# Two 16-head attention stages: who spreads the keys over the heads, and how values and mask enter

## Chip, cores and metric

The kernel is one program on one core of a Trainium2 chip. It is a chain of eight stages (four attention layers, each followed by a feed-forward layer) over 64 sequences of 64 tokens with 256 features; the activations `x` stay in SBUF from the first stage to the last. The metric is the device time of one execution in microseconds. The engines are TensorE (PE), VectorE (DVE), ScalarE (ACT), GpSimd (POOL) and the queue of SyncE (SP), which only issues DMAs.

## The reference, cut to what matters

Two of the attention layers have 16 heads of 16 features and attend from each sequence's 64 tokens to its 64 context tokens. The first (stage 0) quantizes the inputs of its query and output projections to 8 bits; the other (stage 6) has a gate and a mask of context tokens.

```python
# stage 0
q = _w8a8_linear(x, wq, bq).reshape(B, N, H, D).transpose(0, 2, 1, 3)
k = (cond @ wk.T + bk).reshape(B, L, H, D).transpose(0, 2, 1, 3)
v = (cond @ wv.T + bv).reshape(B, L, H, D).transpose(0, 2, 1, 3)
scores = jnp.einsum('bhnd,bhld->bhnl', q, k) * inv_sqrt_d + mask[:, None]
attn = jax.nn.softmax(scores, axis=-1)
o = jnp.einsum('bhnl,bhld->bhnd', attn, v)
...
return _w8a8_linear(o, wo, bo)
# stage 6
attn = jnp.einsum('blhd,bmhd->bhlm', q, k) * scale
attn = jnp.where(memory_mask[:, None, None, :], attn, -jnp.inf)
attn = jax.nn.softmax(attn, axis=-1)
...
out = out @ wo.T
gate = jax.nn.sigmoid(x @ wg.T)
return gate * out
```

## The kernel before

`head_attention_stage` builds both stages: "att8" with `quant=True` (stage 0) and "att32" with `quant=False` (stage 6). The work is cut into 16 units (`NU`) of 256 tokens, which is four sequences, and each unit into two groups (`GU` = 2) of 128 tokens, which is two sequences. All tiles are named `att_...` in the profile.

For a group, `scores_pe` (L2267) makes the scores of all 16 heads in two PSUM banks. It first lays the mask there with two matmuls against the identity (L2278), and then adds four products of queries and keys (L2284). A head has only 16 features, so eight heads at a time share one matmul: the keys `kT` are copied once for each of eight heads and multiplied by the head's 0/1 mask `hmask`. This spread copy is `km`; `keys_pool` (L2150) makes it on POOL in two instructions of 128x2048 elements (L2156). `max_dve` (L2297) takes the row maxima of each head, `exp_act` (L2308) does 16 exponentials, one for a head (L2311), `transpose_pe` (L2314) and `transposed_act` (L2322) turn the result, `apply_pe` (L2331) multiplies it by the values, `result_dve` (L2344) divides by the sums (and, in att8, quantizes: L2365, L2373), `result_pe`, `result_act` and `out_pe` turn it again and multiply by the output weights, and `residual_dve` (L2410) adds it to `x`.

For the unit after, PE makes in between the transposed inputs (`input_pe`, L2168), the keys (`keys_pe`, L2137), the queries (`queries_pe`, L2190 or L2195), the values (`values_pe`, L2227) and in att32 the gate (`gate_pe`, L2255). In att8 `queries_dve` (L2206, L2211) scales the queries on VectorE and `transposed_queries_pe` (L2247) turns them. The context `ctxT` is held twice in a row (its fourth dimension, `j`), so that one values matmul of 128 context rows gives one sequence's values in both halves of the partitions; a unit needs 8 of these matmuls of 256 columns. `values_act` copies them to the block tile `vbd`, even heads from the lower half and odd ones from the upper.

The order of the work is written out by hand, for each engine, in `unit_pe` (L2468), `unit_act` (L2501), `unit_dve` (L2530) and `unit_gp` (L2547). Every engine runs its own list in order; semaphores tie them. The groups overlap in a software pipeline: while the scores of group (t, g) are made, group k = 1 steps back is transposed and applied, k = 2 steps back its result is turned, and k = 3 steps back it is projected and added. The matmuls that make the unit after use two PSUM banks `FB` in turn, six fillings a unit, each waiting until ACT or VectorE has emptied the one before; in att32 the gate is the sixth (`LAST`), after the values. `apply_pe` waits for `y_used` of the group two before, since that group's output stands in the same bank.

`norm_dve` (L2073) normalizes the inputs two units ahead, with powers taken on POOL (`norm_pool`); `bias_pool` (L2404) adds the output bias to `x` in att8 after that. SP loads a unit's context with four DMAs (L2455), two units ahead.

## Time and profile before

| | |
|---|---|
| time, median of 3 runs | 5494.57 us (5493.93 to 5498.47) |
| profiled execution | 5491.58 us, its core's span 5489.8 us |
| PE busy | 4827.4 us, 88% |
| VectorE busy | 2886.1 us, 53% |
| ACT busy | 2072.0 us, 38% |
| POOL busy | 1154.1 us, 21% |
| granted clock of PE, mean | 0.938 |
| L2156 on POOL (the spread, both stages) | 64 instructions, 233.7 us |

| stretch | length | PE busy | VectorE busy | ACT busy | POOL busy | PE clock |
|---|---|---|---|---|---|---|
| att8, 37 to 500 us | 463 us | 347.05 | 348.58 | 205.90 | 150.76 | 0.86 |
| att32, 4370 to 4800 us | 430 us | 378.45 | 187.76 | 215.53 | 148.61 | 0.96 |

The first table is the whole program; the second is the two stages in question. Busy time says how long instructions ran on an engine, and that includes time in which a running instruction was held up. A clock of 1.00 is 2.4 GHz and 0.50 is 1.2 GHz; what stands between is a mean over both. In a timeline row the number in brackets is how long the engine stood idle before the row, and who ended it.

### The profile page before, as it was taken

The numbers are of one execution on the slowest core, as the hardware profiler recorded it, in microseconds if no ns is written. First come the engines' busy times: TensorE is split into PE (matmuls) and PEld (weight loads), VectorE is DVE, ScalarE is ACT, GpSimd is POOL, SyncE is SP. The second block draws the span as 40 slices with busy tenths as digits, with TensorE's granted clock in tenths as the row PEclk, the third lists the DMA queues.
The fourth block names the chain that finished last, engine by engine and source line by source line (L and its number), as shares of the span: only waits on it lengthen the run. The fifth ranks groups of instructions, "written<-read, shape, count | busy, mean of one in ns | idle before, by whom it ended". The sixth has DMA issues, their size and how long they took to land. (4 is left out here: it accounts for less than half of the span.)

```text
span 5489.8 us, 77694 instructions
## 1 busy us (share of the span) xinstructions
PE 4827.4 (88%) x27056; PEld 3829.2 (70%) x27056; DVE 2886.1 (53%) x5919; ACT 2072.0 (38%) x4822; POOL 1154.1 (21%) x758
## 2 busy tenths in 40 slices
PE   5776999998877748999999987999899899889999
PEld 3554899997656626777777776777677666567777
DVE  6776888895553245555555553333333244443333
ACT  3444666663214313333333333332333255443322
POOL 3332323331003300000000001222222243222222
PEclk9887999999989858999999998999899999999999
DMA  2001000000010011000000001000100011010000
GB/s 63 22 21 41 1 0 0 0 0 19 15 41 1 16 48 62 5 4 4 4 1 3 4 5 56 8 8 5 50 12 8 20 24 23 21 42 9 5 8 8
DMA packets 130897, 94.20 MB, mean 17 GB/s; under 512 B 77200, under 2 KB 114160, under 8 KB 130448
## 3 DMA queue, kind: packets, MB, share of 16 engines
q1 hardware_dynamic: 130704, 91.65, 5.6%
q8 instruction: 119, 1.95, 0.2%
q14 instruction: 74, 0.61, 0.0%
HBM read 83.23 MB, written 8.39 MB: 17 GB/s over the span
## 5 line engine op out<-in xcount | busy, mean ns | idle before, releaser
L1152 POOL TENSOR_TENSOR peer_tab<-peer_sims 128x2048 f32<-128x2048 f32 x64 | 245.8, 3860 | 290.0 <-ACT peer_sims L1129 260.4
L1145 ACT ACTIVATE peer_tab<-peer_sims 128x128 f32<-128x128 f32 x1024 | 305.6, 392 | 0.0
L1200 DVE SCALAR_TENSOR_TENSOR peer_tab<-peer_tab,peer_th 128x2048 f32<-128x2048 f32 x128 | 298.3, 2373 | 2.6 <-ACT peer_tab L1145 2.3
L2156 POOL TENSOR_TENSOR att_km<-att_kT,att_hmask 128x2048 f32<-128x2048 f32 x64 | 233.7, 3673 | 247.6 <-ACT att_kT L2146 247.6
L643 DVE TENSOR_TENSOR moe_b<-moe_a,bank 128x512 f32<-128x512 f32 x128 | 88.1, 688 | 370.1 <-PE bank L556 348.3
L631 POOL TENSOR_TENSOR moe_hh_lo<-moe_hh,moe_hh_hi 128x512 fp32r<-128x512 f32 x128 | 171.5, 1340 | 499.0 <-ACT moe_hh_hi L622 479.0
L1217 PE MATMUL bank<-ident,peer_tab 128*128 128x128 f32 x2048 | 247.7, 275 | 23.2 <-DVE peer_tab L1200 23.2
L1217 PEld LDWEIGHTS bank<-ident,peer_tab 128*128 128x128 f32 x2048 | 234.5, 142 | 36.4 <-DVE peer_tab L1200 24.0
L1267 PE MATMUL bank<-peer_wd,peer_hh 128*128 128x256 f32 x1024 | 242.1, 380 | 1.7 <-DVE peer_hh L1258 1.7
L1240 PE MATMUL bank<-peer_hT,peer_wg 128*128 128x256 f32 x1024 | 243.3, 381 | 0.0
L1708 PE MATMUL bank<-mha_wo,mha_oT 128*128 128x256 f32 x1024 | 242.5, 380 | 0.0
L1595 PE MATMUL bank<-mha_wv,mha_hT 128*128 128x512 f32 x512 | 240.4, 592 | 0.0
L643 DVE TENSOR_TENSOR moe2a_b<-moe2a_a,bank 128x512 f32<-128x512 f32 x104 | 71.5, 688 | 295.3 <-PE bank L556 272.6
L631 POOL TENSOR_TENSOR moe2a_hh_lo<-moe2a_hh,moe2a_hh_hi 128x512 fp32r<-128x512 f32 x104 | 141.1, 1356 | 400.1 <-ACT moe2a_hh_hi L622 386.1
L2311 ACT ACTIVATE att_pr<-bank,att_nmax 128x64 f32<-128x64 f32 x1024 | 216.3, 377 | 2.2 <-DVE att_nmax L2306 2.1
L1240 PEld LDWEIGHTS bank<-peer_hT,peer_wg 128*128 128x128 f32 x1024 | 196.4, 192 | 26.2
L643 DVE TENSOR_TENSOR moe2b_b<-moe2b_a,bank 128x512 f32<-128x512 f32 x96 | 66.0, 688 | 272.8 <-PE bank L556 249.9
L631 POOL TENSOR_TENSOR moe2b_hh_lo<-moe2b_hh,moe2b_hh_hi 128x512 fp32r<-128x512 f32 x96 | 130.8, 1362 | 373.2 <-ACT moe2b_hh_hi L622 366.2
L1267 PEld LDWEIGHTS bank<-peer_wd,peer_hh 128*128 128x128 f32 x1024 | 188.7, 191 | 24.1 <-DVE peer_hh L1258 2.3
L1708 PEld LDWEIGHTS bank<-mha_wo,mha_oT 128*128 128x128 f32 x1024 | 185.7, 191 | 19.5
L622 ACT ACTIVATE moe_hh_hi<-moe_hh 128x512 fp32r<-128x512 f32 x128 | 80.9, 632 | 301.2 <-DVE moe_hh L648 301.2
L1616 DVE COPY mha_ks<-bank 128x512 f32<-128x512 f32 x128 | 88.5, 691 | 198.8 <-PE bank L1583 191.5
(485 smaller groups left out, 12675.0 us busy)
## 6 DMA issues: line engine op xcount, KB each, us to landing
att_ctxT<-in_ctxT_dram SPq DMA_DIRECT2D x128, 128.0 KB, 2.5
x<-in_x_dram SPq DMA_DIRECT2D x4, 1024.0 KB, 9.3
lin_ctxT<-in_ctxT_dram SPq DMA_DIRECT2D x16, 256.0 KB, 2.8
mem_ctxT<-in_ctxT_dram SPq DMA_DIRECT2D x16, 256.0 KB, 2.9
mem_ctx<-in_ctx_dram SPq DMA_DIRECT2D x16, 256.0 KB, 3.0
t_scratch<-mha_tT SPq DMA_DIRECT2D x8, 512.0 KB, 2.7
moe2a_hTf<-t_scratch SPq DMA_DIRECT2D x8, 512.0 KB, 3.6
moe2b_hTf<-t_scratch SPq DMA_DIRECT2D x8, 512.0 KB, 3.7
```

The costliest lines, as they stand in the source:

```text
L631: nc.gpsimd.tensor_tensor(out=hhs[1][:, j % 2, :], in0=hh[:, j % 2, :], in1=hhs[0][:, j % 2, :], op=ALU.subtract).then_inc(lo_ready, 1)
L643: nc.vector.tensor_tensor(out=b[:, j % 2, :], in0=a[:, j % 2, :], in1=U[j % 2][:], op=ALU.mult).then_inc(b_ready, 1)
L1145: i = nc.scalar.activation(tab[g][h][:, b * P:(b + 1) * P], sims[:, g, h, P:2 * P], ACT.Identity, bias=sims[:, g, h, b:b + 1])
L1152: nc.gpsimd.tensor_tensor(out=tab[g][h][:].rearrange("p (a b) -> p a b", b=P), in0=sims[:, g, h, P:2 * P].unsqueeze(1).broadcast_to([P, NB ...
L1200: nc.vector.scalar_tensor_tensor(out=tab[g][h][:], in0=tab[g][h][:], scalar=th[:, g, h:h + 1], in1=tab[g][h][:], op0=ALU.is_ge, op1=ALU.mu ...
L1217: i = nc.tensor.matmul(TB[n % 2][:, j * P:(j + 1) * P], tab[g][h][:, blk * P:(blk + 1) * P], core.ident[:], start=(j == 0 and h == 0), sto ...
L1240: i = nc.tensor.matmul(GB[p % 2][:, n * PU:(n + 1) * PU], wg[:, c, blk * P:(blk + 1) * P], hT[par][:, c, :], start=(c == 0), stop=(c == C ...
L1267: i = nc.tensor.matmul(YB[par][:, g * D:(g + 1) * D], hh[:, p % 2, n * PU + g * P:n * PU + (g + 1) * P], wd[:, 2 * p + n, :], start=(p == ...
L1595: i = nc.tensor.matmul(V[:], hT[:, c, g * P:(g + 1) * P], wv[:, c, first * HD:(first + QUAD) * HD], start=(c == 0), stop=(c == C - 1))
L1708: i = nc.tensor.matmul(Y[g // 2][:, (g % 2) * D:(g % 2 + 1) * D], oT[:, s % 2, g * P:(g + 1) * P], wo[:, s, :], start=(s == 0 and g % 2 == ...
L2156: i = nc.gpsimd.tensor_tensor(out=km[par][:, c, :, :, :], in0=kT[:, c, :].rearrange("p (b k) -> p b k", k=S).unsqueeze(2).broadcast_to([P, ...
L2311: i = nc.scalar.activation(pr[g][:, h, :], SB[g][h // H8][:, (h % H8) * S:(h % H8 + 1) * S], ACT.Exp, bias=nmax[:, g, h:h + 1])
```

## The change

Five things change in `head_attention_stage`, for both stages where nothing else is said.

- The spread of the keys leaves POOL. In att8 its first half (`KM_ACT`, features 0 to 127) goes to ACT as 8 activations, one for a head with the head's mask as scale (`spread_act`), and its second half to VectorE as one 128x2048 multiply (`spread_dve`). In att32 both halves go to VectorE.
- The context is held once. One values matmul makes the values of two sequences, one in each half of the partitions, so a unit takes 4 matmuls instead of 8; `values_act` copies them, partly from one half of the partitions to the other, with 8 activations instead of 4. SP issues one context DMA for a unit instead of four.
- In att32 the mask no longer goes through PE. `max_dve` adds it while it moves the scores from PSUM to the SBUF tile `pr` (two adds for a group), then takes one maximum over `pr`, and the exponentials read `pr`.
- The order moves: `queries_pe` stands before `apply_pe` and `result_pe`; `queries_dve` before `result_dve`; the spreads come after `result_act` on ACT and after `result_dve` on VectorE.
- On POOL, `bias_pool` comes before `norm_pool`.

```diff
--- before.py
+++ after.py
...
-    ctxT = [sb(f"ctxT{i}", [P, C, BU, 2, S]) for i in range(2)]
+    ctxT = [sb(f"ctxT{i}", [P, C, UNIT]) for i in range(2)]
...
+    KM_ACT, KM_DVE = ((0,), (1,)) if quant else ((), (0, 1))
+    km_act, km_dve = sem("km_act"), sem("km_dve")
...
-                i = nc.tensor.matmul(F[:, co * UNIT:(co + 1) * UNIT], wkT[:, ci, co * P:(co + 1) * P], ctxT[par][:, ci, :, 0, :],
+                i = nc.tensor.matmul(F[:, co * UNIT:(co + 1) * UNIT], wkT[:, ci, co * P:(co + 1) * P], ctxT[par][:, ci, :],
...
-        if some(t):
-            act.wait_ge(km_ready, t)
+        if some(t * len(KM_DVE)):
+            act.wait_ge(km_dve, t * len(KM_DVE))
+        if some(t * len(KM_ACT)):
+            act.wait_ge(km_act, t * len(KM_ACT))
...
-    def keys_pool(pool, t, par):
-
-        pool.wait_ge(emptied[KEYS % 2], t * 3 + KEYS // 2 + 1)
+    def spread_act(act, t, par):
+
         if some((t - 1) * GU):
-            pool.wait_ge(scored, (t - 1) * GU)
-        for c in range(C):
-            i = nc.gpsimd.tensor_tensor(out=km[par][:, c, :, :, :],
-                                        in0=kT[:, c, :].rearrange("p (b k) -> p b k", k=S).unsqueeze(2).broadcast_to([P, BU, H8, S]),
-                                        in1=hmask[:].unsqueeze(1).unsqueeze(3).broadcast_to([P, BU, H8, S]), op=ALU.mult)
-        i.then_inc(km_ready, 1)
+            act.wait_ge(scored, (t - 1) * GU)
+        act.wait_ge(emptied[KEYS % 2], t * 3 + KEYS // 2 + 1)
+        for c in KM_ACT:
+            for h in range(H8):
+                i = nc.scalar.activation(km[par][:, c, :, h, :], kT[:, c, :].rearrange("p (b k) -> p b k", k=S), ACT.Copy,
+                                         scale=hmask[:, h:h + 1])
+            i.then_inc(km_act, 1)
+
+    def spread_dve(dve, t, par):
+
+        if some((t - 1) * GU):
+            dve.wait_ge(scored, (t - 1) * GU)
+        dve.wait_ge(emptied[KEYS % 2], t * 3 + KEYS // 2 + 1)
+        for c in KM_DVE:
+            nc.vector.tensor_tensor(out=km[par][:, c, :, :, :],
+                                    in0=kT[:, c, :].rearrange("p (b k) -> p b k", k=S).unsqueeze(2).broadcast_to([P, BU, H8, S]),
+                                    in1=hmask[:].unsqueeze(1).unsqueeze(3).broadcast_to([P, BU, H8, S]),
+                                    op=ALU.mult).then_inc(km_dve, 1)
...
-        for b in range(2):
-            for c in range(C):
-                tok = ctxT[par][:, c, 2 * n + b, :, :].rearrange("p j k -> p (j k)")
-                i = nc.tensor.matmul(F[:, b * D:(b + 1) * D], tok, wvT[:, c, :],
-                                     start=(c == 0), stop=(c == C - 1))
+        for c in range(C):
+            i = nc.tensor.matmul(F[:, 0:D], ctxT[par][:, c, n * P:(n + 1) * P], wvT[:, c, :], start=(c == 0), stop=(c == C - 1))
...
-        v = FB[k % 2][:].rearrange("p (b h j d) -> p b h j d", b=2, j=2, d=HD)
-        for j in range(2):
-            i = nc.scalar.activation(vbd[par][64 * j:64 * j + 64, 2 * n:2 * n + 2, :, j, 0:HD], v[64 * j:64 * j + 64, :, :, j, :], ACT.Copy)
+        v = FB[k % 2][:, 0:D].rearrange("p (h j d) -> p h j d", j=2, d=HD)
+        for b in range(2):
+            for j in range(2):
+                i = nc.scalar.activation(vbd[par][64 * j:64 * j + 64, 2 * n + b, :, j, 0:HD], v[64 * b:64 * b + 64, :, j, :], ACT.Copy)
...
-            if not quant:
-                pe.wait_ge(neg_ready, t + 1)
...
-        for c in range(C):
-            nc.tensor.matmul(SB[g][c][:].rearrange("p (h k) -> p h k", k=S), core.ident[:],
-                             add[:, g, :].unsqueeze(1).broadcast_to([P, H8, S]), start=True, stop=False, skip_group_check=True)
+        if quant:
+            for c in range(C):
+                nc.tensor.matmul(SB[g][c][:].rearrange("p (h k) -> p h k", k=S), core.ident[:],
+                                 mask[par][:, g, :].unsqueeze(1).broadcast_to([P, H8, S]), start=True, stop=False, skip_group_check=True)
         if g == 0:
-            pe.wait_ge(km_ready, t + 1)
+            if KM_ACT:
+                pe.wait_ge(km_act, (t + 1) * len(KM_ACT))
+            pe.wait_ge(km_dve, (t + 1) * len(KM_DVE))
         for c in range(C):
             for b in range(2):
                 i = nc.tensor.matmul(SB[g][c][64 * b:64 * b + 64, :], qT[par][:, c, (2 * g + b) * S:(2 * g + b + 1) * S],
-                                     km[par][:, c, 2 * g + b, :, :].rearrange("p h k -> p (h k)"), start=False, stop=(b == 1),
+                                     km[par][:, c, 2 * g + b, :, :].rearrange("p h k -> p (h k)"), start=not quant, stop=(not quant or b == 1),
                                      skip_group_check=True)
...
         kp = keep[:, bass.ds(t * GU, GU), :]
+        m_chain.begin(t)
         nc.vector.tensor_reduce(out=valid[:, par, :], in_=kp, axis=AX.X, op=ALU.max)
-        if some((t - 1) * GU):
-            dve.wait_ge(scored, (t - 1) * GU)
-        nc.vector.tensor_scalar(neg[par][:], kp, 1.0, BIG, ALU.subtract, ALU.mult).then_inc(neg_ready, 1)
-
-    def max_dve(dve, t, g):
+        nc.vector.tensor_scalar(neg[par][:], kp, 1.0, BIG, ALU.subtract, ALU.mult).then_inc(m_chain.sem, 1)
+        dve.wait_ge(m_chain.sem, m_chain.next())
+
...
-        for c in range(C):
-            i = nc.vector.tensor_reduce(out=nmax[:, g, c * H8:(c + 1) * H8], in_=SB[g][c][:].rearrange("p (h k) -> p h k", k=S),
-                                        axis=AX.X, op=ALU.max)
-        i.then_inc(soft_chain.sem, 1)
+        if quant:
+            for c in range(C):
+                i = nc.vector.tensor_reduce(out=nmax[:, g, c * H8:(c + 1) * H8], in_=SB[g][c][:].rearrange("p (h k) -> p h k", k=S),
+                                            axis=AX.X, op=ALU.max)
+            i.then_inc(soft_chain.sem, 1)
+        else:
+            if some(n - 1):
+                dve.wait_ge(pT_ready, n - 1)
+            for c in range(C):
+                i = nc.vector.tensor_tensor(out=pr[g][:, c * H8:(c + 1) * H8, :], in0=SB[g][c][:].rearrange("p (h k) -> p h k", k=S),
+                                            in1=neg[par][:, g, :].unsqueeze(1).broadcast_to([P, H8, S]), op=ALU.add)
+            i.then_inc(s_read, 1)
+            dve.wait_ge(s_read, n + 1)
+            nc.vector.tensor_reduce(out=nmax[:, g, :], in_=pr[g][:], axis=AX.X, op=ALU.max).then_inc(soft_chain.sem, 1)
         dve.wait_ge(soft_chain.sem, soft_chain.next())
...
-            i = nc.scalar.activation(pr[g][:, h, :], SB[g][h // H8][:, (h % H8) * S:(h % H8 + 1) * S], ACT.Exp, bias=nmax[:, g, h:h + 1])
+            s_ = SB[g][h // H8][:, (h % H8) * S:(h % H8 + 1) * S] if quant else pr[g][:, h, :]
+            i = nc.scalar.activation(pr[g][:, h, :], s_, ACT.Exp, bias=nmax[:, g, h:h + 1])
...
-    n_in, n_ctx = 16 * len(loads), 16 * (2 * C + (1 if quant else 0))
+    n_in, n_ctx = 16 * len(loads), 16 * (1 + (1 if quant else 0))
...
-        for c in range(C):
-            for j in range(2):
-                sp.dma_start(ctxT[par][:, c, :, j, :], src[:, c, :].rearrange("p (b k) -> p b k", k=S)).then_inc(ctx_in[par], 16)
+        sp.dma_start(ctxT[par][:], src).then_inc(ctx_in[par], 16)
...
@@ -2478,14 +2500,13 @@
             if g == 0 and exists(t + 1):
                 input_pe(pe, t + 1)
                 keys_pe(pe, t + 1, nxt)
+                queries_pe(pe, t + 1, nxt)
             if g == 1 and quant and exists(t + 1):
                 transposed_queries_pe(pe, t + 1)
             if exists(t1):
                 apply_pe(pe, t1, p1, g1)
             if exists(t2):
                 result_pe(pe, t2, g2)
-            if g == 0 and exists(t + 1):
-                queries_pe(pe, t + 1, nxt)
             if g == 1 and exists(t + 1):
...
-            if g == 0 and not quant and exists(t + 1):
-                q_copy(act, t + 1, nxt, QUERIES)
+            if g == 0 and exists(t + 1):
+                if not quant:
+                    q_copy(act, t + 1, nxt, QUERIES)
+                if KM_ACT:
+                    spread_act(act, t + 1, nxt)
...
             if exists(t):
-                max_dve(dve, t, g)
+                max_dve(dve, t, par, g)
             if exists(t3):
                 residual_dve(dve, t3, p3, g3)
+            if g == 0 and quant and exists(t + 1):
+                queries_dve(dve, t + 1)
             if exists(t1):
                 result_dve(dve, t1, p1, g1)
-            if g == 0 and quant and exists(t + 1):
-                queries_dve(dve, t + 1)
+            if g == 0 and exists(t + 1):
+                spread_dve(dve, t + 1, nxt)
             if g == 1 and not quant and exists(t + 1):
                 neg_dve(dve, t + 1, nxt)
             if g == 1 and exists(t + 2):
                 norm_dve(dve, t + 2)
 
     def unit_gp(pool, t, par):
-        if exists(t + 1):
-            keys_pool(pool, t + 1, 1 - par)
+        if quant and exists(t + 1):
+            bias_pool(pool, t + 1)
         if exists(t + 2):
             norm_pool(pool, t + 2)
-        if quant and exists(t + 1):
-            bias_pool(pool, t + 1)
...
```

## Rows read from the trace of the kernel before

**Rows 1.** Timeline, att8: start us, us, engine, line, instruction, [idle before <- releaser].

```profile
206.83 1.93 PE L2340 MATMUL bank<-att_vbd,att_pT 128*64 128x34 f32 x32 [1.49 <-DVE x L2422]
...
222.54 7.38 POOL L2156 TENSOR_TENSOR att_km<-att_kT,att_hmask 128x2048 f32<-128x2048 f32 x2 [7.47 <-ACT att_kT L2146]
...
222.66 0.60 PE L2190 MATMUL bank<-att_wqT,att_hT 128*128 128x256 bf16 x4
...
223.40 3.04 DVE L2365 TENSOR_TENSOR att_o<-att_o,att_bv 128x256 f32<-128x256 f32 x1
...
232.54 1.09 PE L2247 MATMUL bank<-ident,att_qf 128*128 128x128 f32 x4 [4.49 <-DVE att_qf L2211]
...
235.11 1.93 PE L2340 MATMUL bank<-att_vbd,att_pT 128*64 128x34 f32 x32 [1.49 <-DVE x L2422]
```

**Rows 2.** VectorE groups, 80 to 448 us: line, instruction, count, busy us, mean ns, idle.

```profile
L2365 DVE TENSOR_TENSOR att_o<-att_o,att_bv 128x256 f32<-128x256 f32 x27 | 44.7, 1655 | 0.9
...
L2088 DVE SCALAR_TENSOR_TENSOR att_xn<-x,att_mv,att_rstd 128x256 f32<-128x256 f32 x26 | 24.5, 980 | 10.6 <-POOL att_rstd L2122 10.6
...
L2350 DVE RECIPROCAL att_rsum<-bank 128x16 f32<-128x16 f32 x27 | 7.0, 258 | 51.6 <-PE bank L2340 51.6
```

**Rows 3.** Stretches of 1 us, att8: busy times; third from the end PEclk.

```profile
230.00:231.00 1.00, 0.00 (x0) 0.00 (x0) 0.87 (x3) 0.00 (x0) 0.00 (x0) 0.65 0.87 197
...
240.00:241.00 1.00, 1.00 (x5) 0.86 (x4) 0.85 (x5) 0.18 (x1) 0.00 (x0) 0.73 0.00 0
```

**Rows 4.** Timeline, att32: PE's order through a unit, and two VectorE rows.

```profile
4522.04 1.88 PE L2278 MATMUL bank<-att_neg,ident 128*128 128x512 f32 x4
...
4530.41 3.62 PE L2227 MATMUL bank<-att_wvT,att_ctxT 128*128 128x256 f32 x16
...
4533.87 1.89 PE L2255 MATMUL bank<-att_wgT,att_hT 128*128 128x256 f32 x8
...
4535.60 1.88 PE L2278 MATMUL bank<-att_neg,ident 128*128 128x512 f32 x4
...
4537.41 1.94 PE L2284 MATMUL bank<-att_km,att_qT 128*64 128x512 f32 x8
...
4539.27 1.13 PE L2401 MATMUL bank<-att_woT,att_oT 128*128 128x256 f32 x4
...
4539.39 1.29 DVE L2302 TENSOR_REDUCE att_nmax<-bank 128x8 f32<-128x512 f32 x2 [2.99 <-PE bank L2284]
...
4541.12 0.60 PE L2168 MATMUL bank<-ident,att_xn 128*128 128x128 f32 x4
...
4541.53 0.43 DVE L2426 SCALAR_TENSOR_TENSOR x<-att_y,x 128x256 f32 x1 [0.17 <-DVE att_y L2424]
4541.55 1.89 PE L2137 MATMUL bank<-att_ctxT,att_wkT 128*128 128x256 f32 x8
...
4543.38 1.13 PE L2340 MATMUL bank<-att_vbd,att_pT 128*64 128x34 f32 x32
...
4544.71 1.89 PE L2195 MATMUL bank<-att_hT,att_wqT 128*128 128x256 f32 x8
...
4546.44 1.88 PE L2278 MATMUL bank<-att_neg,ident 128*128 128x512 f32 x4
```

**Rows 5.** VectorE groups, 4420 to 4736 us (13 units of att32).

```profile
L2353 DVE TENSOR_SCALAR att_rsum<-att_rsum,att_valid 128x16 f32<-128x16 f32 x26 | 43.5, 1671 | 0.9
L2302 DVE TENSOR_REDUCE att_nmax<-bank 128x8 f32<-128x512 f32 x52 | 33.5, 686 | 61.4 <-PE bank L2284 61.4
...
L2350 DVE RECIPROCAL att_rsum<-bank 128x16 f32<-128x16 f32 x26 | 6.7, 258 | 60.8 <-PE bank L2340 60.8
```

**Rows 6.** Groups of the whole program: prices of forms that the change adds.

```profile
L172 DVE TENSOR_TENSOR ffn_wg_lo<-ffn_dq_wg,ffn_wg_hi 128x2048 fp32r<-128x2048 f32 x1 | 2.3, 2293 | 2.0 <-ACT ffn_wg_hi L177 2.0
...
L1145 ACT ACTIVATE peer_tab<-peer_sims 128x128 f32<-128x128 f32 x1024 | 305.6, 392 | 0.0
L2311 ACT ACTIVATE att_pr<-bank,att_nmax 128x64 f32<-128x64 f32 x1024 | 216.3, 377 | 2.2 <-DVE att_nmax L2306 2.1
```

More of the change, by code:

```diff
@@ L2026, in head_attention_stage @@
     emptied = [sem(f"emptied{i}") for i in range(2)]
-    km_ready, scored, m_ready, e_ready = (sem(n) for n in ("km_ready", "scored", "m_ready", "e_ready"))
+    scored, s_read, m_ready, e_ready = (sem(n) for n in ("scored", "s_read", "m_ready", "e_ready"))
     pT_ready, pTs_ready, o_ready = (sem(n) for n in ("pT_ready", "pTs_ready", "o_ready"))
@@ L2049, in head_attention_stage @@
         neg, valid = [sb(f"neg{i}", [P, GU, S]) for i in range(2)], sb("valid", [P, 2, GU])
-        neg_ready = sem("neg_ready")
         ms_ready, ms_eps, r1_raw, rr_ready = sem("ms_ready"), sem("ms_eps"), sem("r1_raw"), sem("rr_ready")
         norm_chain = Chain(sem("norm_chain"), 3)
+        m_chain = Chain(sem("m_chain"), 1)
     INPUT, KEYS, QUERIES = range(3)
@@ L2268, in scores_pe @@
         n = t * GU + g
-        add = mask[par] if quant else neg[par]
         QK = LAST if quant else QUERIES
         if g == 0:
-            if not quant:
-                pe.wait_ge(neg_ready, t + 1)
             pe.wait_ge(emptied[QK % 2], t * 3 + QK // 2 + 1)
@@ L2291, in neg_dve, with max_dve @@
         kp = keep[:, bass.ds(t * GU, GU), :]
+        m_chain.begin(t)
         nc.vector.tensor_reduce(out=valid[:, par, :], in_=kp, axis=AX.X, op=ALU.max)
-        if some((t - 1) * GU):
-            dve.wait_ge(scored, (t - 1) * GU)
-        nc.vector.tensor_scalar(neg[par][:], kp, 1.0, BIG, ALU.subtract, ALU.mult).then_inc(neg_ready, 1)
-    def max_dve(dve, t, g):
+        nc.vector.tensor_scalar(neg[par][:], kp, 1.0, BIG, ALU.subtract, ALU.mult).then_inc(m_chain.sem, 1)
+        dve.wait_ge(m_chain.sem, m_chain.next())
+    def max_dve(dve, t, par, g):
         n = t * GU + g
```

## Prediction

> **What bounds the kernel now.** I read the views in this order: the page's slices (TensorE 88% busy overall, but 50 to 90% in the first stage), then the timeline of one unit in each of the two stages the change touches, then the groups of VectorE (DVE) in steady units, then the granted clock around TensorE's (PE's) pauses. Only these two stages change: "att8" (16 units) and "att32" (16 units).
>
> In att8 a unit takes 235.11 - 206.83 = 28.28 us. PE stands idle 4.49 us for `att_qf` and 1.49 us for `x`, both from VectorE [rows 1]. VectorE is late because GpSimd (POOL) spreads the keys meanwhile: the 128x256 add of L2365, met 0.9 us after L2156 started, took 3.04 us [rows 1]. Its mean is 1.655 us [rows 2], though 128x256 elements should take 0.42 us: an estimate from 2048 elements in 2.293 us and 512 in 0.686 us [rows 5, 6], 1.05 ns an element. L2373 is hit in the same way; L2088 runs into POOL's bias add, mean 0.98 for 0.42 by the same estimate. VectorE itself is held up by PE only at L2350, 51.6 us in 27 calls, so 3.8 us a unit [rows 2]. So att8 is a VectorE queue of some 24.5 us with two short waits. PE's pauses bring it down to the lower of its two clock levels: the 1 us stretch of the drop shows 0.65, the one of the rise 0.73 [rows 3], and 235.11 to 240.7 ran at 1.2 GHz, although PE was dense from 235.11.
>
> In att32 a unit takes 4546.44 - 4522.04 = 24.40 us [rows 4] and PE runs nearly without a gap. VectorE waits for PE 61.4 + 60.8 us in 13 units, so 9.4 us a unit, and loses 2.9 us to POOL at L2353 (43.5 us in 26 calls, where a 128x16 operation needs about 0.23) [rows 5]. So att32 is bound by PE, and work moved from POOL and PE to VectorE lands on an engine with some 12.1 us of work (24.40 - 9.4 - 2.9).
>
> **att8, part by part.** (1) POOL's spread goes (2 x 3.67 us). The stalls of L2365 and L2373 go with it: 2 x 2 x (1.655 - 0.42) = 4.9 us a unit. The bias add now starts right behind `xn_ready`, beside the maxima, which read PSUM: L2088's 2 x 0.56 = 1.1 us a unit goes too. (2) Half the spread (128x2048) lands on VectorE. The nearest row is the two-input 128x2048 form, 2.293 us [rows 6]. Bounds: 1.2 us if it ran at two elements a cycle, 3.7 us if it took what POOL takes [rows 1]. I take 2.3. Both inputs are broadcast views, which I price at nothing. (3) The other half is 8 activations of 128x256 on ScalarE (ACT): L1145's 128 elements cost 305.6/1024 = 0.30 us each [rows 6], so 0.4 for 256 (estimate, 0.83 ns an element more), 3.2 us a unit. They stand ahead of the copy of the transposed scores. Counted from the end of scores(t,0): keys copied at 3, exponentials 3.4, a result copy 0.4, spread 3.2, transposed copy 1.1, so 11.2; the step that needs it, `apply`, also needs VectorE's second residual, which ends at 12.4 (2.57, queries 1.8, result 3.2, spread 2.3, 2.57). Hidden; without that cover up to 3.2 us a unit. (4) Values: 4 matmuls of 256 columns in place of 8, 3.46 to 1.73 us of PE (start to start, 4530.41 to 4533.87) [rows 4]; ACT gets 8 pieces in place of 4, +0.8 us a unit at most. PE has room: nothing. (5) Queries move ahead of `apply`, and VectorE's query step ahead of its result step, so `qf` no longer comes behind the stalls and the 4.49 us pause goes. (6) 4 context DMAs become 1; nobody waits for them in a steady unit: nothing.
>
> Sum: 28.28 - 3.8 - 4.9 - 1.1 + 2.3 = 20.8 us of VectorE queue. Two waits remain. The first is before the query step: PE's input 0.43, keys 1.83 [rows 4], queries 0.60 [rows 1] and 0.1 of signalling against VectorE's maximum and residual, 2.57 us (4539.39 to 4541.53 + 0.43) [rows 4]: 0.4 us. The second is `apply`, which can't begin before VectorE's residual: 0.3 of signalling plus 1.1 us (1.13 at full clock, 1.93 at the lower, [rows 1, 4]), 1.4 to 2.3. So 22.6 to 23.5 us. PE still has two pauses of about 2 to 2.6 us a unit, and some will cost clock just when VectorE waits for input, keys and queries (up to 2.9 us more). I take 24.0. Fifteen such steps: 15 x 4.3 = 64 us gained (range 35 to 84).
>
> **att32, part by part.** Removed from PE: 4 mask matmuls, 2 x 1.81 us, and half the values, 1.73 [rows 4], leaving some 19 us less its old pause, about 17.6. Added to VectorE: both halves of the spread, 2 x 2.29; four adds of the mask, each 0.69 (priced by the 128x512 maximum that also reads PSUM, 0.686 [rows 5]; bounds 0.5 and 1.1); the one wait behind them 0.1. The maximum over 1024 SBUF elements costs what two over 512 PSUM elements did. The stall of L2353 goes. VectorE's queue is 12.1 + 4.6 + 2.8 + 0.2 = 19.7 us.
>
> But queue and PE take turns here. Count from the moment scores(t,0) are done. PE: output and transposes 1.85, input 0.43, keys 1.83, queries 1.73, apply 1.05, with 0.3 of signalling: 7.2 us [rows 4]. Only then can VectorE do result(t-1,1), about 1.0, then both spreads 4.6, then the maximum and residual of the second group, 2.57 + 1.4 = 3.95: 16.7. Behind that residual stands `apply(t,0)` on PE, and behind `apply` everything else. PE had finished its second scores and transposes by about 11: a pause of over 5 us. Then follow at full clock 0.2, apply and result 1.33, values 1.73, gate 1.73, scores 1.86. That alone gives 23.6. ACT however starts the second exponentials only when that maximum is ready (15.7); 16 of them cost 3.4 us from PSUM (216.3/1024 each), under 4.8 by L1145 [rows 6], and from SBUF I take 3.9; a result copy of 256 elements about 0.4, the first values copy 4 x 0.3 = 1.2, and only then is the bank free for `gate`: 21.2 + 1.73 + 1.86 = 24.8 us.
>
> With a pause of 5 us I expect the lower clock. In att8 4.49 us idle gave it, and it lasted 5.6 us into dense work [rows 1, 3]. Apply to values then take twice 3.06, until 23.0, and gate and scores follow mostly at the upper level: 26.6 us, 2.2 more than now. Fifteen steps: 33 us lost (range: 7 lost at full clock, 60 lost).
>
> The Trainium skill (TensorE: Matmul & The Clock Gate, section on HAM oscillation in real kernels) says that a loop which leaves TensorE waiting in each pass restarts each pass at the lower clock. This case's trace agrees at the 4.49 us pause of att8. By that rule att32's unit is the 26.6 us, without it the 24.8. The skill (VectorE: DVE Perf Modes, section on SBUF-source operations) also gives ScalarE 52 cycles more for a source in SBUF than in PSUM; by it the 16 exponentials would take 3.4 + 0.7 = 4.1 us, an estimate, where I took 3.9, and the full-clock unit 25.0.
>
> Heads and tails of the stages: the first spread gets shorter (3 us each), the last units get the adds on their chain (3 us). Nothing. Total: 5491.6 - 64 + 33 = 5460.6 for the profiled execution, which lay 3.0 us under the median of the runs. Forecast 5463.
>
> **Rivals.**
> A. The clock stays up in att32, or the pause is shorter than counted. Unit 24.4 to 24.8 us, stage 0 to 7 us lost; total 5430. For it: full clock through all of att32 now, and pauses of 1.4 us do no harm. Against: my pause is 5 us. Chance 0.20.
> B. Both stages do better: in att32 the VectorE chain sets the pace at 23.6 or less, because the adds or the spread are cheaper than their rows. Total 5405. Chance 0.06.
> C. Slower. In att32 the pause keeps PE at the lower level through gate and scores as well, in every unit, and the long loop of VectorE and PE feeds itself: 26.6 + 3.6 = 30.2 us less the part that is hidden, so 29 to 30; 15 x 5.2 = 78 us lost against 64 gained: 5508. It decides from a unit of 28.7 us on. For it: two engines in turns, and att8 now, with a similar share of pauses, loses 5 to 10 us a unit to the lower level. Against: there the level rose within dense work shorter than what att32 will have. Chance 0.13.
> D. The change doesn't do what it says in att8: the freed VectorE only swaps POOL's stalls for PE's lower clock and waits (26.5 us a unit), att32 as forecast: 5497. For it: the loop att8 has between VectorE and PE is kept. Against: the queue itself is 3.6 us shorter, and the longest pause is gone. Chance 0.10.
> My forecast: 0.51, by itself 5438 to 5485.
>
> **How the numbers follow.** 0.2% of this time is 11 us, about what a measurement of this kernel can tell from no change. Faster than 5484: nearly all of my case (0.48), A, B, a little of D: 0.76. Within: 0.03 of my case, most of D's rest: 0.11. Slower: C and nothing else: 0.13. The range leaves out B's lower half and C's upper half: 5408 to 5510.
>
> **What would show it.** att8: unit near 24, L2365 and L2373 near 0.42 and 0.48, no `att_qf` wait of 4 us, and the 128x2048 multiply near 2.3 us. att32: VectorE busy near 80%, PE pausing about 5 us before L2340's successor with `x` as releaser, a mean clock clearly below 1.00, unit 26 to 27. Wrong if the spread on VectorE costs over 3 us, if att32 keeps clock 1.00, or if att8's unit stays above 26.

## The result, and the profile after

| | before | after |
|---|---|---|
| time, median | 5496.52 us (5493.93 to 5498.85, 4 runs) | 5440.88 us (5438.93 to 5444.32, 4 runs) |
| profiled execution, its span | 5491.58 us, 5489.8 us | 5442.19 us, 5440.4 us |
| att8 with its head and tail | 457.8 us | 382.5 us |
| the stages between | 3886.7 us | 3890.8 us |
| att32 with its head and tail | 406.8 us | 426.8 us |

The changed kernel takes 0.99 of the time before (95% interval 0.9882 to 0.9917), 56 us less. In the two profiled executions the difference is 49.4 us of span: att8 gives 75.3, att32 costs 20.0, the rest 5.9. The stage lengths are differences of starts: from a stage's first `xn` (L2090 in att8, at 36.8 before and 37.3 after; L2117 in att32) to the first statistics of the stage behind it. The view of who reads `x`, after (form, count, least/mean/greatest ns, first to last start):

```profile
L1048 DVE BATCH_NORM_STATS2 peer_stats<-x x32: 407/416/427, 419.8 to 1137.6; 128x6 f32 x24, 128x6 f32<-128x256 f32 x8
...
L2117 DVE SCALAR_TENSOR_TENSOR att_xn<-x,att_mv,att_rr x32: 477/482/486, 4310.6 to 4677.9; 128x256 f32<-128x256 f32 x32
L287 DVE BATCH_NORM_STATS2 moe_stats<-x x32: 407/409/427, 4737.4 to 5276.9; 128x6 f32<-128x256 f32 x16, 128x6 f32 x16
```

419.8 - 37.3 is att8, 4737.4 - 4310.6 is att32. The same rows give the lengths of all kernels below.

The timeline of one unit of att8, after, which answers to [rows 1]:

```profile
203.69 1.73 PE L2364 MATMUL bank<-att_vbd,att_pT 128*64 128x34 f32 x32 [3.05 <-DVE x L2446]
...
205.46 0.26 DVE L2374 RECIPROCAL att_rsum<-bank 128x16 f32<-128x16 f32 x1 [2.12 <-PE bank L2364]
...
217.03 0.88 DVE L2221 SCALAR_TENSOR_TENSOR att_qf<-bank,att_sx,att_swq 128x256 f32<-128x256 f32 x2 [0.40 <-PE bank L2205]
...
219.41 0.42 DVE L2389 TENSOR_TENSOR att_o<-att_o,att_bv 128x256 f32<-128x256 f32 x1
...
220.71 0.48 DVE L2397 SCALAR_TENSOR_TENSOR att_o<-att_o,att_rso,att_fixed 128x256 f32<-128x256 f32 x1
220.72 3.42 ACT L2161 ACTIVATE att_km<-att_kT,att_hmask 128x256 f32<-128x256 f32 x8
...
221.57 2.28 DVE L2171 TENSOR_TENSOR att_km<-att_kT,att_hmask 128x2048 f32<-128x2048 f32 x1
...
223.91 1.20 ACT L2352 ACTIVATE att_pT<-bank 128x512 f32<-128x512 f32 x2
...
226.58 1.13 PE L2364 MATMUL bank<-att_vbd,att_pT 128*64 128x34 f32 x32 [3.03 <-DVE x L2446]
...
227.76 3.62 PE L2240 MATMUL bank<-att_wvT,att_ctxT 128*128 128x256 f32 x8
```

The unit is 226.58 - 203.69 = 22.89 us. The adds that took 3 us beside POOL take 0.42, half the spread takes 2.28 on VectorE and 3.42 on ACT. VectorE stands still for PE twice, 2.12 us for `apply` (1.51 in the next unit, where `apply` ran at the full clock) and 0.40 for the queries. From 80 to 380 us it waits 25.0 us for `apply` in 27 groups, so 1.9 us a unit (group: count, busy us, mean ns, idle before):

```profile
L2374 DVE RECIPROCAL att_rsum<-bank 128x16 f32<-128x16 f32 x27 | 6.9, 254 | 25.0 <-PE bank L2364 25.0
```

The same view of one unit of att32, after, which answers to [rows 4]:

```profile
4472.62 1.94 PE L2297 MATMUL bank<-att_km,att_qT 128*64 128x512 f32 x8
...
4481.63 0.26 DVE L2374 RECIPROCAL att_rsum<-bank 128x16 f32<-128x16 f32 x1 [3.13 <-PE bank L2364]
...
4482.62 4.48 DVE L2171 TENSOR_TENSOR att_km<-att_kT,att_hmask 128x2048 f32<-128x2048 f32 x2
...
4487.02 1.28 DVE L2323 TENSOR_TENSOR att_pr<-bank,att_neg 128x512 f32<-128x512 f32 x2
...
4489.80 3.93 ACT L2335 ACTIVATE att_pr<-att_pr,att_nmax 128x64 f32<-128x64 f32 x16 [2.93 <-DVE att_nmax L2329]
...
4491.01 1.88 PE L2364 MATMUL bank<-att_vbd,att_pT 128*64 128x34 f32 x32 [5.26 <-DVE x L2450]
...
4493.30 2.50 PE L2240 MATMUL bank<-att_wvT,att_ctxT 128*128 128x256 f32 x8
...
4494.97 2.30 ACT L2252 ACTIVATE att_vbd<-bank 64x128 f32<-64x128 f32 x8 [0.98 <-PE bank L2240]
...
4496.16 1.99 PE L2268 MATMUL bank<-att_wgT,att_hT 128*128 128x256 f32 x8 [0.36 <-ACT att_vbd L2252]
...
4498.09 1.94 PE L2297 MATMUL bank<-att_km,att_qT 128*64 128x512 f32 x8
```

Here the unit is 4498.09 - 4472.62 = 25.47 us, against 24.40. PE stands 5.26 us for `x`, because VectorE makes both halves of the spread (4.48 us), then the adds and the maximum, before it reaches that residual. Stretches of 1 us around the pause, and one of 220 us of the stage (length, busy us of PE, PE's weight loads, VectorE, ACT and POOL with their instructions, granted clock of PE, DMA share, GB/s):

```profile
4490.00:4491.00 1.00, 0.00 (x0) 0.02 (x1) 0.51 (x2) 1.00 (x5) 0.00 (x0) 1.00 0.00 0
4491.00:4492.00 1.00, 0.99 (x21) 1.00 (x22) 0.00 (x0) 1.00 (x6) 0.00 (x0) 0.55 0.00 0
...
4494.00:4495.00 1.00, 1.00 (x5) 0.80 (x5) 0.86 (x5) 0.03 (x1) 0.00 (x0) 0.74 0.00 0
...
4420.00:4640.00 220.00, 176.13 (x1254) 125.83 (x1252) 135.33 (x263) 130.06 (x447) 15.71 (x35) 0.90 0.04 11
```

The clock still stands at 1.00 (2.4 GHz) at the end of the pause, falls to the lower level as the work comes back (0.55 in that microsecond), and rises halfway through the one from 4494 (0.74): some 3.4 us. This happens in every steady unit: twelve of them, counted from `gate` to `gate`, take 25.3 to 25.8 us.

### The profile page after: what moved, and what is told of

It is laid out like the page before. It is cut to its first block and busy times, and to the rows that moved or that the text cites. A ratio compares the mean times of both kernels' runs of the same rounds, so it can differ in the third digit from the quotient of the medians.

```text
span 5440.4 us, 77052 instructions
## 1 busy us (share of the span) xinstructions
PE 4748.9 (87%) x26672; PEld 3774.5 (69%) x26672; DVE 2897.5 (53%) x5999; ACT 2160.3 (40%) x5078; POOL 920.4 (17%) x694
## 5 line engine op out<-in xcount | busy, mean ns | idle before, releaser
L1217 PE MATMUL bank<-ident,peer_tab 128*128 128x128 f32 x2048 | 247.9, 275 | 24.4 <-DVE peer_tab L1200 24.4
L2364 PE MATMUL bank<-att_vbd,att_pT 128*64 128x34 f32 x2048 | 91.7, 253 | 127.1 <-DVE x L2450 62.6
L1609 ACT ACTIVATE mha_vs<-bank 128x512 f32<-128x512 f32 x128 | 76.4, 597 | 297.6 <-PE bank L1595 297.6
```

Source lines behind the costliest of these rows:

```text
L1217: i = nc.tensor.matmul(TB[n % 2][:, j * P:(j + 1) * P], tab[g][h][:, blk * P:(blk + 1) * P], core.ident[:], start=(j == 0 and h == 0), sto ...
L2364: i = nc.tensor.matmul(OB[g][64 * b:64 * b + 64, p * 2 * HV:(p + 1) * 2 * HV], pT[:, p, 64 * b:64 * b + 64], vbd[par][:, 2 * g + b, p, :, ...
```

## The experiments

All numbers are medians with their span, ratios are to the kernel before with their 95% interval. "After" has 5440.9 us.

**e1: the old att32 beside the new att8.** The stage function of before is kept under another name and called for att32.

```diff
-head_attention_stage(core, "att32", quant=False)
+head_attention_stage_before(core, "att32", quant=False)
```

> The changed kernel, with the second stage (att32) exactly as it was before the change; att8 changed. My account of the two traces is that att8 gained 75 us and att32 lost 20 us. If the stages are independent: att32 back at 407 us from 427, the whole 20 us faster than the changed kernel, about 5421. If some of att8's gain was only moved (a debt paid in later stages), the whole stays at 5435 to 5441.

5418.39 us (5416.37 to 5421.67), ratio 0.9863 (0.9847 to 0.988). att8 382.4, att32 409.0 us. att8 keeps its gain when att32 is the old one, so the stages can be taken one by one, as in all that follows. The median is 22 us below after's. In the profiled executions the span is 25 us shorter: 18 us are att32's, 5 lie between the stages (3885.6 us for 3890.8) and 2 behind them, which the edit doesn't touch.

**e2: att32's mask back on PE.** Four matmuls against the identity again, the maxima and exponentials straight from PSUM; the spread stays on VectorE.

```diff
-        if quant:
+        if True:
             for c in range(C):
                 nc.tensor.matmul(SB[g][c][:]..., core.ident[:],
-                                 mask[par][:, g, :]...
+                                 (mask if quant else neg)[par][:, g, :]...
```

> The changed kernel with att32's mask put back on PE (two matmuls a group) and the maxima and exponentials reading PSUM; the spread stays on VectorE. Loop theory (apply waits for VectorE's residual, which stands behind result, both spreads and the second maximum): the loop loses the adds, 1.4 us, but PE has 1.8 us more in the chain from gate to scores; PE's pause shrinks from 5.3 to about 2.5 us and the clock stays up; unit 24.0 to 24.7 against 25.47, 12 to 22 us faster. ScalarE theory (what costs is that exponentials read SBUF, 3.93 for 3.38 us): 0.55 us a unit, 9 us faster, with the pause as long as before. PE theory (any PE work given back costs): 3.6 us a unit, 58 us slower.

5430.06 us (5426.58 to 5434.96), ratio 0.9886 (0.987 to 0.9903); att32 418.7, 8 us less than after, and the whole 11 us less, just under what was expected. PE's pause halves as expected, but the clock holds in some units only. Timeline of e2, `apply` and `gate` of two units, and two stretches of the stage:

```profile
4430.88 1.13 PE L2367 MATMUL bank<-att_vbd,att_pT 128*64 128x34 f32 x32 [2.29 <-DVE x L2453]
...
4434.47 1.99 PE L2268 MATMUL bank<-att_wgT,att_hT 128*128 128x256 f32 x8 [0.37 <-ACT att_vbd L2252]
...
4581.76 1.13 PE L2367 MATMUL bank<-att_vbd,att_pT 128*64 128x34 f32 x32 [2.28 <-DVE x L2453]
...
4586.44 1.96 PE L2268 MATMUL bank<-att_wgT,att_hT 128*128 128x256 f32 x8
```

```profile
4362.00:4458.00 96.00, 85.89 (x607) 56.34 (x606) 51.94 (x111) 54.77 (x206) 6.60 (x15) 1.00 0.04 12
4460.00:4660.00 200.00, 180.99 (x1202) 120.48 (x1200) 103.25 (x221) 109.15 (x407) 13.90 (x31) 0.94 0.04 10
```

From `apply` to `gate` it is 3.59 us in the first unit and 4.68 in the second, behind the same pause. Counted from `gate` to `gate`, the four units of the first stretch take 24.2 to 24.4 us and the eight of the second 25.4 to 25.8. The first is what e4 takes below with the mask on VectorE and the clock at 1.00 (24.2 to 24.4), the second what after takes (25.3 to 25.8). So at an equal clock the place of the mask is worth nothing that can be measured: the mask's 1.88 us come back on PE in the loop and cancel what VectorE and ACT save. Most of the 8 us are the units in which the clock stayed up, five of them, 1.3 us each. Why it stayed up in those and not in the others, with pauses of 2.2 to 2.3 us in both, isn't shown.

**e3: att32's spread back on POOL**, the mask stays on VectorE. **e5: the same in att8**, all else new.

```diff
+    ON_POOL = not quant        # e5: ON_POOL = quant
+    if ON_POOL:
+        KM_ACT, KM_DVE = (), (0, 1)
...
+        for c in range(C):
+            nc.gpsimd.tensor_tensor(out=km[par][:, c, :, :, :], in0=kT..., in1=hmask..., op=ALU.mult)
```

> The changed kernel with att32's spread put back on POOL; the mask stays on VectorE. Loop theory: 4.6 us leave VectorE's part of the loop, some 1 to 2 us of stalls beside POOL come back (the 128x16 multiply, the residual with two SBUF inputs); the pause of PE shrinks to 1 to 2 us, the unit to 22.6 to 23.5, 30 to 45 us faster than the changed kernel, and att32 below its 407 us of before. ScalarE theory: the chain exponentials, result copy, values copy, gate, scores is as long as in the changed kernel, so within 5 us of it. Port theory (keeping POOL off SBUF is what matters): 30 us slower or more.

5390.91 us (5384.01 to 5393.82), ratio 0.9809 (0.9792 to 0.9825). att32 falls to 378.5 us, 28 us under the kernel before and 48 under after: slightly more than the loop theory said. Timeline of e3:

```profile
4480.39 7.21 POOL L2174 TENSOR_TENSOR att_km<-att_kT,att_hmask 128x2048 f32<-128x2048 f32 x2 [6.90 <-ACT att_kT L2153]
...
4482.65 1.40 DVE L2391 TENSOR_SCALAR att_rsum<-att_rsum,att_valid 128x16 f32<-128x16 f32 x1
...
4484.59 1.29 DVE L2337 TENSOR_TENSOR att_pr<-bank,att_neg 128x512 f32<-128x512 f32 x2
...
4488.87 1.93 PE L2378 MATMUL bank<-att_vbd,att_pT 128*64 128x34 f32 x32 [2.39 <-DVE x L2464]
```

POOL's 7.2 us lie beside VectorE's work. Of that one 128x16 operation with both inputs in SBUF is held up (1.40 us for 0.23 elsewhere), and by 0.3 us the 128x16 negation behind the maxima (L2343); the adds of the mask read PSUM and SBUF and take 1.29 us for two, as without POOL. The pause is 2.39 us and the unit 4495.85 - 4473.42 = 22.43. With the spread back on POOL att32 is also 30 us shorter than the old stage in e1 (409.0), so the rest of the change is a gain there. e7 prices the values; what the moved queries give in att32, and the mask's place beside a spread on POOL, have no run of their own.

> The changed kernel with att8's whole spread back on POOL; order, values and bias add as changed, att32 as changed. Stall theory (att8's gain is that POOL no longer holds up VectorE's two-input operations): VectorE loses its 2.3 us multiply but gets back two or three stalls of 1.5 to 3.3 us a unit; unit 24.5 to 27 against 22.89, 25 to 60 us slower than the changed kernel. Load theory (VectorE is simply the busiest engine of att8, the stalls are hidden by the new order): unit 20.6 to 22, 15 to 37 us faster. att32's run with the spread on POOL gained, so the second is to be taken seriously.

5503.0 us (5498.64 to 5511.03), ratio 1.0015 (1.0006 to 1.0025): att8 443.0 us, 60.5 more than after. Timeline of e5:

```profile
243.16 7.64 POOL L2174 TENSOR_TENSOR att_km<-att_kT,att_hmask 128x2048 f32<-128x2048 f32 x2 [7.26 <-ACT att_kT L2153]
...
243.55 3.78 DVE L2240 TENSOR_TENSOR att_qf<-att_qf,att_bq 128x512 f32<-128x512 f32 x1 [0.15 <-DVE att_qf L2235]
...
247.99 3.10 DVE L2403 TENSOR_TENSOR att_o<-att_o,att_bv 128x256 f32<-128x256 f32 x1
...
255.66 1.93 PE L2378 MATMUL bank<-att_vbd,att_pT 128*64 128x34 f32 x32 [6.63 <-DVE x L2460]
```

The stalls are back in the new order (3.78 us for the 0.69 of a 128x512 add, 3.10 for 0.42), and PE waits 6.63 us. The two stalls are 5.8 us a unit and the multiply that left VectorE 2.3, so 3.5 of the 4.0 us by which a unit grew (26.8 us from spread to spread). So of att8's 75 us, 60 are the spread that left POOL. The Trainium skill (SBUF — State Buffer, section on who interferes with whom) says that a VectorE instruction with two SBUF inputs contends with a GpSimd instruction that reads SBUF, and one with at most one such input, outside its two-port modes, doesn't. The rows of e5 agree for the first, the adds of e3 for the second. L2343 of e3 has one input in SBUF and took 299 ns on the mean for 175 after; no run here shows in which mode it ran.

**e4: fill the pause of att32.** Four idle matmuls of 512 columns, whose results serve nothing, into the free score banks, ahead of `apply(t,0)`.

```diff
+        if g == 0 and not quant:
+            for r in range(4):
+                nc.tensor.matmul(SB[g][r % 2][:], core.ident[:], wkT[:]..., start=True, stop=True, ...)
```

> The changed kernel with four matmuls of 512 columns that serve nothing, put in att32 ahead of apply(t, 0), into a scores bank that is free just then, in PE's pause of 5.3 us; nothing else differs. If the lower clock after the pause costs: apply back from 1.88 to 1.13 us, values copy no longer waiting 0.98 us for its matmuls, 0.6 to 1.0 us a unit, 10 to 16 us faster, granted clock of the stage near 1.00. If ScalarE's chain hides the lower clock: within 3 us. If the loop's length alone decides: within 3 us as well, with the clock at 1.00.

5422.25 us (5420.09 to 5425.36), ratio 0.9869 (0.9852 to 0.9885); att32 410.1, 17 us less. Timeline of e4:

```profile
4483.71 3.70 PE L2360 MATMUL bank<-att_wkT,ident 128*128 128x512 f32 x8 [1.18 <-ACT att_pT L2352]
...
4487.68 1.13 PE L2367 MATMUL bank<-att_vbd,att_pT 128*64 128x34 f32 x32 [0.28 <-DVE x L2453]
...
4491.85 1.99 PE L2268 MATMUL bank<-att_wgT,att_hT 128*128 128x256 f32 x8 [0.94 <-ACT att_vbd L2252]
```

The clock reads 1.00 over 220 us of the stage where it read 0.90. The unit is 24.37 us, so the lower level costs att32 1.1 us a unit (1.3 on the mean of the steady units, 25.6 and 24.3) and the longer loop nothing: at full clock the new att32 is as long as the old. After shows where the 1.1 goes: ACT waits 0.98 us for the slow values.

**e6: att8's old order.** Queries behind `apply` on PE, and VectorE's query step behind its result step.

```diff
                 keys_pe(pe, t + 1, nxt)
-                queries_pe(pe, t + 1, nxt)
...
+            if g == 0 and exists(t + 1):
+                queries_pe(pe, t + 1, nxt)
```

> The changed kernel with att8's query steps in the order of before: PE's queries behind apply and result, VectorE's query step behind its result step (ahead of the spread). If the moved order carried the gain: the pause of PE for the scaled queries comes back, 2 to 4 us a unit, 30 to 60 us slower. If the order matters little once the stalls are gone (VectorE does the same work, and only the 0.4 us wait for the queries moves): within 8 us of the changed kernel.

5452.24 us (5450.38 to 5453.85), ratio 0.9918 (0.9901 to 0.9935); att8 397.6 us, 15 more. Neither theory: the order is worth 11 to 15 us, about 1 us a unit. No long pause for `qf` comes back, and none is there in e5, with the stalls and the new order: the pause of before took both. The timeline of e6 has instead:

```profile
244.90 0.26 DVE L2374 RECIPROCAL att_rsum<-bank 128x16 f32<-128x16 f32 x1 [1.52 <-PE bank L2364]
...
254.55 1.93 PE L2364 MATMUL bank<-att_vbd,att_pT 128*64 128x34 f32 x32 [3.81 <-DVE x L2446]
```

VectorE waits 1.52 us for a product that in the new order is made while it works on the queries. The new order fills a hole in VectorE's queue. The three steps that were taken back one at a time, 60 by e5, 15 here and 5 by e7, add up to 80 us and not to 75, so they overlap a little.

**e7: values as before in both stages**, eight matmuls, four context DMAs and two copies of 64x256 for each pair of sequences.

```diff
-            i = nc.tensor.matmul(F[:, 0:D], ctxT[par][:, c, n * P:(n + 1) * P], wvT[:, c, :], ...)
+            for b in range(2): ... i = nc.tensor.matmul(F[:, b * D:(b + 1) * D], tok, wvT[:, c, :], ...)
```

> The changed kernel with the values made as before in both stages: context held twice, 8 matmuls and 4 copies a unit, 4 context DMAs. PE gets 1.73 us a unit more at full clock. In att8 VectorE sets the pace and PE has pauses: 0 to 5 us in the stage. In att32 the first half of the values takes 0.87 us more (1.7 at the lower clock) ahead of the copy that frees the gate's bank, while the copy itself is 0.35 us shorter: 0.5 to 1.4 us a unit, 8 to 22 us. Together 8 to 27 us slower. If PE's work is hidden in both: within 3 us.

5465.3 us (5464.03 to 5467.82), ratio 0.9944 (0.9928 to 0.9961); att8 +4.6, att32 +21.0 us, both within what was expected. In att32 values stand on the path behind the pause, at the lower level, and ACT's copy waits for them (timeline of e7):

```profile
4505.59 4.97 PE L2242 MATMUL bank<-att_wvT,att_ctxT 128*128 128x256 f32 x16
...
4508.87 0.79 ACT L2254 ACTIVATE att_vbd<-bank 64x256 f32<-64x256 f32 x2 [2.65 <-PE bank L2242]
```

4.97 us for 2.50: the halved values save 1.3 us a unit of att32, without which the stage would have lost 41 us rather than 20.

**e8: att32 with the spread split between ACT and VectorE as in att8, mask on PE.** The edit of e2, and `KM_ACT, KM_DVE = (0,), (1,)` for both stages.

> The changed kernel with att32 spread as att8 is (first half on ScalarE, second on VectorE) and with its mask back on PE. VectorE's part of the loop loses 2.3 us against the run with the mask on PE and the spread on VectorE. Loop theory with VectorE alone: unit 22 to 22.7, the whole near 5395. But ScalarE gets 3.4 us a unit ahead of the copy of the transposed scores and of the second exponentials, and PE has 1.8 us more between gate and scores: if that chain sets the pace, the unit stays at 24.0 to 24.7 and the whole at 5420 to 5430.

5423.31 us (5422.84 to 5426.29), ratio 0.9868 (0.9852 to 0.9885); att32 410.9 us. The numbers are those of the case in which ACT's chain takes over, but not by the reason given. Timeline of e8, and its group of transposed copies from 4420 to 4640 us (9 units):

```profile
4480.45 3.43 ACT L2161 ACTIVATE att_km<-att_kT,att_hmask 128x256 f32<-128x256 f32 x8
...
4485.81 3.40 ACT L2338 ACTIVATE att_pr<-bank,att_nmax 128x64 f32<-128x64 f32 x16
...
4486.16 1.13 PE L2367 MATMUL bank<-att_vbd,att_pT 128*64 128x34 f32 x32 [1.36 <-ACT att_pT L2355]
...
4490.46 1.99 PE L2268 MATMUL bank<-att_wgT,att_hT 128*128 128x256 f32 x8 [1.08 <-ACT att_vbd L2252]
```

```profile
L2355 ACT ACTIVATE att_pT<-bank 128x512 f32<-128x512 f32 x36 | 19.5, 594 | 53.0 <-PE bank L2345 53.0
```

VectorE had the maximum ready at 4484.4, but ACT starts the exponentials at 4485.8; PE waits for ACT at `apply` and at `gate`. ACT isn't late by its half of the spread: that ends at 4483.9, and ACT then stands idle for 0.96 us until PE's transposes are done, in each unit (53.0 us in 9 units, 5.0 and 0.96 us in each). The transposes come late because the mask is laid on PE ahead of the scores. So what sets the pace is a loop of PE and ACT: transposes, their copy, exponentials, values copy, `gate`, mask, scores. Against the units of e2 at full clock (24.2 to 24.4 us) e8's take 24.1 to 24.2, so 2.3 us less on VectorE gain some 0.2.

**e9: e3 with one idle matmul of 512 columns ahead of att32's `apply(t,0)`. e10: the same in att8 too.**

```diff
+        if g == 0 and not quant:   # e10: if g == 0
+            for r in range(1):
+                nc.tensor.matmul(SB[g][r % 2][:], core.ident[:], wkT[:]..., ...)
```

> The run with att32's spread on POOL, with one matmul of 512 columns that serves nothing in att32's pause ahead of apply(t, 0). That run kept a pause of 2.4 us and a lower clock behind it: apply 1.93 for 1.13 us, and the values copy waited 0.88 us for its matmuls. If both go, as four such matmuls did in the longer pause: unit 21.4 to 21.8 against 22.43, 10 to 16 us faster than that run, near 5377. If one matmul is too little to hold the clock: within 3 us of it.

5378.16 us (5376.97 to 5382.74), ratio 0.9786 (0.977 to 0.9802), 13 us under e3: the fastest of all. The stretch of 4420 to 4640 us, e3 and then e9 (columns as in the stretches above):

```profile
4420.00:4640.00 220.00, 194.41 (x1432) 139.01 (x1432) 126.01 (x288) 149.66 (x516) 88.07 (x60) 0.92 0.04 11
```

```profile
4420.00:4640.00 220.00, 197.69 (x1493) 133.16 (x1490) 132.58 (x298) 153.79 (x533) 94.27 (x62) 1.00 0.04 11
```

0.92 becomes 1.00, and the unit goes from 22.43 to 21.44 us. Two units of e3's own trace ran at 1.00, and they took 21.4 us too; its others, in the middle of the stage, 22.1 to 22.6.

> As the run before it, and the same one matmul in att8's pause too. att8's queue on VectorE includes the wait for apply, which takes 1.73 to 1.93 us at the lower clock in some units and 1.13 in others: 0 to 0.8 us a unit, 3 to 10 us faster than the run with it in att32 alone. If VectorE's queue hides it: the same within 2 us.

5381.73 us (5380.35 to 5384.4), ratio 0.9792 (0.9776 to 0.9808). att8 takes 385.4 us for 382.6: nothing gained, within a few us. PE's groups in att8, 80 to 380 us, e9 and then e10 (busy us, mean ns, idle before):

```profile
L2254 PE MATMUL bank<-att_wvT,att_ctxT 128*128 128x256 f32 x104 | 42.1, 577 | 0.0
...
L2142 PE MATMUL bank<-att_ctxT,att_wkT 128*128 128x256 f32 x104 | 25.5, 388 | 0.0
```

```profile
L2142 PE MATMUL bank<-att_ctxT,att_wkT 128*128 128x256 f32 x107 | 33.1, 462 | 0.0
L2254 PE MATMUL bank<-att_wvT,att_ctxT 128*128 128x256 f32 x104 | 27.1, 407 | 0.0
```

Values got faster (407 ns for 577), keys slower (462 for 388). Values are made while VectorE works through its queue, and cost nothing there at the lower level; the keys are ahead of the queries, for which VectorE waits. The lower level moved from a covered place to an uncovered one. Why it moved isn't settled.

## Why the prediction was right or wrong

**The whole.** The direction and the range held, and the order of the two effects too: 75 us gained and 20 lost against 64 and 33 forecast. The profiled execution took 5442.2 us where 5460.6 was forecast, 18.4 less: att8 11 less, att32 13 less, the rest 6 more. Both stages missed mostly by the same kind of term, what the clock costs. The median, 5440.9 us, lies 3 us above the lower end of what my own case allowed (5438 to 5485).

**att8, the sum: right.** 22.6 to 23.5 us was worked out and 22.89 measured. L2389 and L2397 take 0.42 and 0.48, the multiply 2.28 for 2.3, the two waits 0.40 and 2.12 (1.9 on the mean) for 0.4 and 1.4 to 2.3, and ACT's 3.42 us of spread stay hidden: `pT` is ready at 225.1, `x` at 226.2. The cause of the stalls is shown by e5. L2088's successor, L2090, no longer meets the bias add (0.88 us for two).

**att8, the clock: mis-sized.** The step that failed is "I take 24.0", an addition of 0.5 to 1.4 us for clock lost where VectorE waits. In the unit that starts at 226.58 the level fell at about 227.9, after the pause (stretches of 1 us: 1.00 at 226, 0.93 at 227, 0.50 at 228), and stayed low over values (3.62 us for 8 matmuls), which VectorE's queue hides. e10 shows the other side: taking the lower level from `apply` and values gains nothing. Fifteen steps of 4.3 us were forecast; 75.3/15 = 5.0 came, a little under the 5.4 of the units shown, since the unit of before that the sum starts from (28.28) is longer than most: spreads of before start 27.2 to 28.2 us apart, 27.8 on the mean.

**att8, the order: a smaller reason than given.** I put the end of the 4.49 us pause down to the queries' new place; by e6 it doesn't come without the stalls, by e5 not with them in the new order, and the order is worth 1 us a unit.

**att32, the loop: right.** From the end of scores(t,0), 4474.5: result at 7.1 (7.2 forecast), spreads 4.48 (4.6), the second group's maximum at 15.2 (15.7), its residual at 16.15 (16.7), exponentials 3.93 (3.9), pause 5.26 (over 5) with `x` as releaser. An add took 0.68 us, as priced, but two back to back span 1.28, and the whole of maximum and residual took 3.63, not 3.95. At full clock the unit is 24.37 (e4) where ACT's chain gave 24.8. That ACT comes next is shown by e4 and e8, where `gate` waits for its copy; in e8 ACT itself waits for PE's transposes.

**att32, the clock: right in kind, mis-sized.** The step that failed is "apply to values then take twice 3.06, until 23.0". I took from att8 that the lower level lasts 5.6 us into dense work (the 0.73 of [rows 3] puts its end at 240.5, so 5.4); here it lasted 3.4, and values were done at 21.3. So it cost 1.1 us a unit (e4) and not 1.8, from a base 0.4 lower: 25.47 for 26.6. The Trainium skill (TensorE: Matmul & The Clock Gate, section on HAM oscillation in real kernels) says that such a loop restarts each pass at the lower level; the stretches of after agree, those of e2 in part only, where four passes with a pause of 2.2 to 2.3 us ran at 1.00.

**What was read wrongly ahead.** VectorE "near 80%" in att32 has no working behind it and is wrong: 135.3 us of 220, 62%. Values "nothing", said of att8, is 4.6 us by e7: small, but more than the 2 us by which that stage varies between kernels that share it. For att32 the sum did have the halved values behind `apply`, and e7 gives them 21 us. Rival C said that att8 lost 5 to 10 us a unit to the lower level; by stretches of 1 us the level was low for 10.2 us of the unit shown, and PE worked for 6.5 of them, so at most 3.3 were lost.

**The rivals.** A asked for a clock that stays up; it fell in each unit seen (0.90 over the stage). B needed an att32 of 23.6 us a unit or less, C one of 28.7 or more, D an att8 of some 26.5; all three are excluded. The remaining 5.9 us outside the two stages, 4.1 of them between, stay open. They aren't chance alone: the stage of linear attention, from its first statistics to those of the next, took 319.7 us before, 324.6 after, and 322.8 to 324.2 in the ten experiments, none of which touches it.

## What to carry to other kernels

Where an operation keeps VectorE waiting beside POOL, count the SBUF inputs of what stands next to it: the same spread on POOL cost att8 60 us and gained att32 48, since there it leaves VectorE 4.5 us of the loop, and only one operation of 128x16 with two SBUF inputs falls beside it. An engine with room on average can still be the long part of a loop of two engines taking turns, so draw the loop from one shared point before moving work to the one that seems free. Compare two variants at the same granted clock before crediting an edit: e2's 8 us were the clock's, and the mask's place gave nothing. A clock loss is priced only where the slow instructions stand on the path; filling a pause with one idle matmul was worth 13 us in one stage and nothing in the other.

## What the runs showed of the hardware

- The lower clock level came late after the change: 5.3 us after the start of the pause in att32, with PE at work again, and in att8 at about 227.9, 4.3 us after the start of a pause of 3.03 us. It lasted some 3.4 us in both (att8: 0.50 until 231 and 0.86 in the microsecond after). In att8 before it came 2.3 us after the start of the pause of 4.49 us, with PE idle, and stayed for 5.4 us of dense work. In e2 pauses of 2.2 to 2.3 us were followed by full clock in some units and by the lower level in others.
- An operation of VectorE that was held up beside POOL's multiply ended soon after the POOL instruction that ran beside it, and within its own undisturbed time (0.23 us for 128x16, 0.42 for 128x256, 0.69 for 128x512): at 4484.05 us with POOL's end at 4484.0 in e3, at 247.33 with 246.8 and 251.09 with 250.8 in e5, at 226.44 with 226.2 before [rows 1]. How much one loses is thus set by where in that instruction it falls: 128x16 elements lost 1.2 us in e3, and 2.9 before at 4520.45 us (L2353). The POOL instruction behind a held operation took longer in its turn, 4.07 us for 3.62 in e5.
- 16 exponentials of 128x64 took 3.93 us from SBUF (after) and 3.40 from PSUM (e8), 33 ns more each.
- Multiplying 128x2048 elements with both inputs as broadcast views took 2.28 us on VectorE, as much as the two-input form of that size before (2.293, [rows 6]), 3.42 as eight activations on ACT, and 3.6 on POOL in e3.
